# Gating the experts' rows at their copy-out, and six macro tiles of the shared expert inside the last three attention steps

## The reference, cut to what matters

```python
x = x + attention(layernorm(x))          # 16 heads of 8, window 64, rotary positions
xf = layernorm(x)                        # what follows works on xf
shared = (silu(xf @ sg) * (xf @ su)) @ sd
# router: 4 of 8 groups, then 4 of 32 experts for each token, by l2-normed centroids and a bias
gates = softmax(top_scores)              # 4 gates a token
# each expert takes at most 640 (token, choice) pairs, in token order; later ones are dropped (keep = 0)
h = silu(buf @ wg[e]) * (buf @ wu[e])    # buf: the 640 slots of expert e
out_e = h @ wd[e]
routed[token] += out_e[slot] * gate * keep
x = x + shared + routed
```

## Time and profile before

| what | value |
|---|---|
| median of 3 runs | 727.87 us (726.16 to 729.05) |
| span of the profiled execution, which is its own time here | 904.6 us, mean granted TensorE clock 0.829 |
| busy: PE, PEld, DVE, ACT, POOL | 724.0, 563.5, 534.0, 360.9, 415.1 us |
| instructions | 24570 |
| stages of the profiled execution | start to 63 us; attention to 514.4; drain steps 33, 34, 35 to 525.8, 532.8, 539.4; two macro tiles to 552.8; experts to 837.2; two late macro tiles beside the last scatter to 847.4; results and four macro tiles to 904.6 |

### The profile page before, as it was taken

One profiled execution on the slowest core, in us unless ns is written; L12 is line 12 of the kernel. 1 busy time (PEld: TensorE's weight loads), 2 busy tenths in 40 slices (PEclk: granted clock), 3 DMA queues, 4 the chain that ended last, 5 costly groups with the idle time before them and its releaser, 6 DMA issues.

```text
span 904.6 us, 24570 instructions
## 1 busy us (share of the span) xinstructions
PE 724.0 (80%) x7521; PEld 563.5 (62%) x7521; DVE 534.0 (59%) x2192; ACT 360.9 (40%) x853; POOL 415.1 (46%) x548
## 2 busy tenths in 40 slices
PE   3798888988978788898888858888888888877960
PEld 1565656665646565575665637777777777777540
DVE  3476756556577676656666656545454454543598
ACT  4465544454455445444454423332323232322200
POOL 4125343353343434334344350555555555556555
PEclk9698776676798878767788859999999999998985
DMA  8991000000000000000000002423233333421355
GB/s 268 358 390 35 14 20 15 12 23 12 12 22 10 20 9 15 10 7 14 6 7 6 6 8 84 125 76 105 76 114 107 114 115 103 126 75 32 122 182 167
DMA packets 52338, 68.37 MB, mean 76 GB/s; under 512 B 9505, under 2 KB 31807, under 8 KB 52304
## 3 DMA queue, kind: packets, MB, share of 16 engines
q1 hardware_dynamic: 38240, 53.56, 18.4%
q0 software_dynamic: 9216, 11.97, 4.4%
q10 hardware_dynamic: 4848, 2.40, 0.9%
HBM read 34.89 MB, written 39.99 MB: 83 GB/s over the span
## 4 chain that ended last, share of the span: by engine, by line
PE 52%; another core or an unknown queue 19%; issue 10%; DVE 10%; ACT 6%; POOL 1%; ACTq 1%; DVEq 1%; POOLq 0%
PE bank L693 9%; PE bank L864 7%; PE bank L680 6%; PE bank L674 5%; PE bank L663 5%; PE bank L657 3%; PE bank L701 3%; DVE x_all L1246 3%; DVE mx L1044 2%; PE bank L733 2%; ACT hact L607 2%; PE bank L817 2%; PE bank L756 1%; PE bank L747 1%
## 5 line engine op out<-in xcount | busy, mean ns | idle before, releaser
L463 POOL DMA_INDIRECT pair_results<-yout,yidx x160 | 157.2, 982 | 143.4 <-ACT yout L625 104.0
L447 POOL DMA_INDIRECT expert_slots<-xfe,sidx x128 | 127.0, 992 | 141.5 <-DVE sidx L1148 108.3
L864 PE MATMUL bank<-xgT_parts,wgu_parts 128*128 128x320 f32 x768 | 147.2, 344 | 46.4 <-ACT hact L607 46.4
L864 PEld LDWEIGHTS bank<-xgT_parts,wgu_parts 128*128 128x128 f32 x768 | 125.9, 208 | 57.3 <-ACT hact L607 50.3
L519 ACT ACTIVATE pt<-bank 128x512 f32<-128x512 f32 x128 | 76.2, 596 | 182.2 <-PE bank L680 164.9
L1259 DVE TENSOR_TENSOR hact<-hact,bank 128x320 f32<-128x320 f32 x128 | 57.1, 481 | 140.2 <-ACT hact L607 133.1
L1044 DVE TENSOR_REDUCE mx<-bank 128x4 f32<-128x512 f32 x128 | 87.3, 683 | 32.5 <-PE bank L663 19.7
L421 POOL TENSOR_TENSOR pout<-pin,mhalf 128x3 f32<-128x3 f32 (+2 forms) x36 | 29.9, 830 | 127.4 <-DVE pin L970 127.4
L890 PE MATMUL bank<-wdn,hact 128*128 128x128 f32 x640 | 82.7, 288 | 2.3 <-issue 2.3
L890 PEld LDWEIGHTS bank<-wdn,hact 128*128 128x128 f32 x640 | 82.5, 207 | 2.5 <-issue 2.5
L623 ACT COPY yout<-bank 128x512 f32<-128x512 f32 x32 | 18.7, 585 | 162.2 <-remote 151.0
(11 more groups left out here) (148 smaller groups left out, 1335.1 us busy)
## 6 DMA issues: line engine op xcount, KB each, us to landing
expert_slots<-fill SPq DMA_DIRECT2D x32, 322.5 KB, 6.5
xg<-expert_slots SPq DMA_DIRECT2D x32, 322.5 KB
pair_results<-rload SPq DMA_DIRECT2D x32, 256.0 KB
rload<-pair_results SPq DMA_DIRECT2D x16, 512.0 KB, 4.0
wgu<-in_L_ffn_wg_dram SPq DMA_DIRECT2D x32, 128.0 KB
wgu<-in_L_ffn_wu_dram SPq DMA_DIRECT2D x32, 128.0 KB
wdn<-in_L_ffn_wd_dram SPq DMA_DIRECT2D x32, 128.0 KB
pair_results<-yout,yidx POOLq DMA_INDIRECT x160
```

The lines of the kernel that those rows point to most:

```text
L447: g.indirect_dma_start(out=slots_d, out_offset=bass.IndirectOffsetOnAxis(ap=sidx[:, tr.b, k:k + 1], axis=0), in_=xfe[:, tr.b, k, :], in_of ...
L463: g.indirect_dma_start(out=pairs_d, out_offset=bass.IndirectOffsetOnAxis(ap=yidx[:, c, j:j + 1], axis=0), in_=yout[:, c, j, :], in_offset= ...
L864: last = mm(bank[2 + 2 * w + h][:, 0:CH], wgu_parts[:, e.b, wp, w, h * P:(h + 1) * P], xgT_parts[:, e.b, xp, ch * CH:(ch + 1) * CH], start ...
```

## The change

The gate moves from the end of the kernel to the experts' copy-out. The rows in the slot buffer get one more column (ROW = 130), the gate of the pair, which VectorE writes where it wrote the table of gates before; the scatter to the slots waits for it. In an expert's step ScalarE does five activations of 128x128 with the gate as scale per row in place of two copies, each with its own semaphore count; GpSimd waits, in front of each of its five scatters, for that one part. The copy of the pair numbers (and now gates) on VectorE moves from the head of the step to its end. At the end GpSimd does one addition of 128x512 a pair of tiles and VectorE two of 128x256.

Six of the eight macro tiles move into the drain, two in each of the steps 33 to 35, with single PSUM banks for gate (0), up (1) and down (5), placed between the attention and routing work of each engine. The other two stand where the early ones stood. None is left behind the experts.

```diff
...
 SPAN = P + WIN
-ROW = D + 1
+ROW = D + 2
 OOB = float(1 << 20)
...
 CH = cap // 2
-SHARED_EARLY = 2
+SHARED_DRAIN = 6
 NR = 8
-CSTEPS = 5
-COMB_EARLY = 4 * (N // 512 - SHARED_EARLY - 2)
+CSTEPS = 2
...
 xfT_all = sb("xfT_all", [P, N])
-gates = sb("gates", [P, NT, TOPK])
...
 yout = sb("yout", [P, 2, ST, D])
-ypair = sb("ypair", [P, 2, ST])
+ypair = sb("ypair", [P, 2, ST, 2])
...
 rload = sb("rload", [P, NR, TOPK, D])
-gates_late = sb("gates_late", [P, NR, 2])
...
       tile_of((m - 1) // 2, (m - 1) % 2) if m > start else None)
+def drain_macro(tau, i):
+  if isinstance(tau, int) and NT < tau < NT + 4:
+    return tile_of(tau - NT - 1, i)
+  return None
...
     sp.dma_start(xg[:, c].rearrange("p j c -> p (j c)"), slots_v[e]).then_inc(xg_arrived[c], 16)
-  sp.wait_ge(S.fill_done, 2)
+  sp.wait_ge(S.fill_done, 3)
...
   g.memset(fill[:, :, 0:D], 0.0).then_inc(S.fill_done, 1)
-  g.memset(fill[:, :, D:ROW], OOB).then_inc(S.fill_done, 1)
+  g.memset(fill[:, :, D:D + 1], OOB).then_inc(S.fill_done, 1)
+  g.memset(fill[:, :, D + 1:ROW], 0.0).then_inc(S.fill_done, 1)
...
       hold(pool)
-      g.tensor_copy(xfe[:, tw.b, :, D:ROW], pair[:, bass.ds(tw.n, 1), :].rearrange("p o k -> p k o"))\
+      g.tensor_copy(xfe[:, tw.b, :, D:D + 1], pair[:, bass.ds(tw.n, 1), :].rearrange("p o k -> p k o"))\
...
       pool.wait_ge(S.xf_copied, tr.n + 1)
+      pool.wait_ge(S.gate_done, 2 * tr.n + 2)
...
       pool.wait_ge(S.yidx_ready, e + 1)
-      pool.wait_ge(S.y_evac, 2 * e + 2)
-      hold(pool)
       for j in range(ST):
+        pool.wait_ge(S.y_evac, ST * e + (j + 1))
+        hold(pool)
...
           oob_is_err=False).then_inc(y_sent[c], 16)
-  pool.wait_ge(S.gate_done, 2 * NT)
...
       tiles = slice(2 * c, 2 * c + 2)
-      g.tensor_copy(gates_late[:, tiles, :], gates[:, bass.ds(2 * q, 2), 2:TOPK])\
-      .then_inc(S.late_gates, 1)
       pool.wait_ge(r_arrived[c], 16 * (i + 1))
-      pool.wait_ge(S.late_gates, q + 1)
       hold(pool)
-      g.tensor_tensor(rload[:, tiles, 2:TOPK, :], rload[:, tiles, 2:TOPK, :],
-              gates_late[:, tiles, :].unsqueeze(3).broadcast_to([P, 2, 2, D]), ALU.mult)\
-      .then_inc(S.late_gated, 1)
-      pool.wait_ge(S.late_gated, q + 1)
-      g.tensor_tensor(rload[:, tiles, 2, :], rload[:, tiles, 2, :], rload[:, tiles, 3, :], ALU.add)\
-      .then_inc(S.late_sum, 1)
+      g.tensor_tensor(rload[:, tiles, 0:2, :], rload[:, tiles, 0:2, :], rload[:, tiles, 2:TOPK, :],
+              ALU.add).then_inc(S.half_sum, 1)
...
   def step(tau, tn, tf, tp, ts, tw, tr):
+    def drain_silu(i, h):
+      m = drain_macro(tau, i)
+      if m is not None:
+        act.wait_ge(S.sh_gu, 4 * m.n + (2 * h + 1))
+        wait(act, S.sh_down, m.n - 1)
+        a.activation(sact[:, m.b, h], bank[0][:, :], ACT.Silu).then_inc(S.sh_act, 1)
...
       a.copy(xfT[:, tr.b], bank[4][:, 3 * D:3 * D + P]).then_inc(S.xfT_evac, 1)
+    drain_silu(0, 0)
...
       .then_inc(S.xf_copied, 1)
+    drain_silu(0, 1)
...
       a.copy(oT[:, tw.b], bank[3][:, 0:P]).then_inc(S.oT_evac, 1)
+    drain_silu(1, 0)
     exponentials(0)
...
     exponentials(3)
+    drain_silu(1, 1)
...
         a.activation(sact[:, m.b, h], bank[h][:, :], ACT.Silu).then_inc(S.sh_act, 1)
-  shared_steps(shared_step, 0, SHARED_EARLY)
+  shared_steps(shared_step, SHARED_DRAIN, N // 512)
...
       wait(act, y_sent[ed.b], 16 * ST * ed.half)
-      a.copy(yout[:, ed.b, 0:4], bank[6][:, :].rearrange("p (j d) -> p j d", d=D))\
-      .then_inc(S.y_evac, 1)
-      a.copy(yout[:, ed.b, 4:ST], bank[7][:, 0:D].rearrange("p (j d) -> p j d", d=D))\
-      .then_inc(S.y_evac, 1)
+      act.wait_ge(S.ypair_ready, ed.n + 1)
+      hold(act)
+      for j in range(ST):
+        a.activation(yout[:, ed.b, j], bank[6 + j // 4][:, j % 4 * D:(j % 4 + 1) * D], ACT.Copy,
+              scale=ypair[:, ed.b, j, 1:2]).then_inc(S.y_evac, 1)
...
   lagged_steps(act, expert_step, NE, True)
-  shared_steps(shared_step, SHARED_EARLY, N // 512)
...
       last.then_inc(S.qkT_done, 1)
+    def drain_gate_up(i, h):
+      m = drain_macro(tau, i)
+      if m is None:
+        return
+      cols = slice(h * P, (h + 1) * P)
+      if m.n == 0 and h == 0:
+        pe.wait_ge(S.w_loaded, 16 * 3)
+        pe.wait_ge(S.p1_reduced, NU * NT)
+        pe.wait_ge(S.mT_evac, NT)
+        pe.wait_ge(S.qT_evac, NT)
+      pe.wait_ge(S.xfT_kept, 4 * m.n + 4)
+      wait(pe, S.sh_act, 2 * m.n + h)
+      mm(bank[0][:, :], sgw[:, cols], xfT_all[:, bass.ts(m.n, 512)], start=True, stop=True)\
+       .then_inc(S.sh_gu, 1)
+      wait(pe, S.sh_mul, 2 * m.n + h)
+      mm(bank[1][:, :], suw[:, cols], xfT_all[:, bass.ts(m.n, 512)], start=True, stop=True)\
+       .then_inc(S.sh_gu, 1)
+    def drain_down(i):
+      m = drain_macro(tau, i)
+      if m is None:
+        return
+      pe.wait_ge(S.sh_mul, 2 * m.n + 2)
+      wait(pe, S.sh_added, m.n)
+      for j in range(4):
+        for h in range(2):
+          last = mm(bank[5][:, j * D:(j + 1) * D], sact[:, m.b, h, j * P:(j + 1) * P], sdw[:, h, :],
+               start=(h == 0), stop=(h == 1))
+      last.then_inc(S.sh_down, 1)
...
        .then_inc(S.xfT_done, 1)
+    drain_gate_up(0, 0)
...
         pe.wait_ge(S.centT_evac, 1)
+    drain_gate_up(0, 1)
...
       first_scores(0)
+    drain_gate_up(1, 0)
...
       mm(bank[3][:, P:2 * P], oT[:, tw.b], wout[:, :], start=True, stop=True).then_inc(S.wout_done, 1)
+    drain_down(0)
...
       second_scores(3)
+    drain_gate_up(1, 1)
...
       last.then_inc(S.pvT_done, 1)
+    drain_down(1)
   attention_steps(pe, step)
-  pe.wait_ge(S.w_loaded, 16 * 3)
...
       last.then_inc(S.sh_down, 1)
-  shared_steps(shared_step, 0, SHARED_EARLY)
-  pe.wait_ge(S.sh_added, SHARED_EARLY)
+  pe.wait_ge(S.sh_act, 2 * SHARED_DRAIN)
+  pe.wait_ge(S.sh_mul, 2 * SHARED_DRAIN)
+  shared_steps(shared_step, SHARED_DRAIN, N // 512)
+  pe.wait_ge(S.sh_added, N // 512)
...
       pe.wait_ge(S.h_mul, 4 * ed.n + 4)
-      wait(pe, S.y_evac, 2 * ed.n)
+      wait(pe, S.y_evac, ST * ed.n)
...
   lagged_steps(pe, expert_step, NE, True)
-  pe.wait_ge(S.h_act, 4 * NE)
-  pe.wait_ge(S.h_mul, 4 * NE)
-  shared_steps(shared_step, SHARED_EARLY, N // 512)
...
       dve.wait_ge(S.gate_done, 2 * tr.n + 1)
-      v.scalar_tensor_tensor(gates[:, bass.ds(tr.n, 1), :].rearrange("p o k -> p (o k)"), ex4[:, tr.b],
-                 exr[:, :], keep[:, :], ALU.mult, ALU.mult).then_inc(S.gate_done, 1)
+      v.tensor_scalar(xfe[:, tr.b, :, D + 1], ex4[:, tr.b], exr[:, :], None, ALU.mult)\
+      .then_inc(S.gate_done, 1)
+    def drain_times(i, h):
+      m = drain_macro(tau, i)
+      if m is not None:
+        dve.wait_ge(S.sh_act, 2 * m.n + (h + 1))
+        dve.wait_ge(S.sh_gu, 4 * m.n + (2 * h + 2))
+        v.tensor_tensor(sact[:, m.b, h], sact[:, m.b, h], bank[1][:, :], ALU.mult)\
+        .then_inc(S.sh_mul, 1)
+    def drain_add(i):
+      m = drain_macro(tau, i)
+      if m is not None:
+        dve.wait_ge(S.sh_down, m.n + 1)
+        xs = x_all[:, bass.ds(4 * m.n, 4), :]
+        v.tensor_tensor(xs, xs, bank[5][:, :].rearrange("p (t d) -> p t d", d=D), ALU.add)\
+        .then_inc(S.sh_added, 1)
     def at(tile, operation, *args):
...
     at(tr, masked_a)
+    drain_times(0, 0)
     at(tp, maxima, 0)
     at(tr, masked_b)
+    drain_times(0, 1)
     at(tw, add_attention)
...
     at(tr, marks_b)
+    drain_times(1, 0)
     at(tw, length_a)
...
     at(tp, maxima, 3)
+    drain_add(0)
     at(tr, positions_a)
...
     at(tr, slots_c)
+    drain_times(1, 1)
+    drain_add(1)
...
       .then_inc(S.sh_added, 1)
-  shared_steps(shared_step, 0, SHARED_EARLY)
+  shared_steps(shared_step, SHARED_DRAIN, N // 512)
   def combine(q, c, turn):
-    dve.wait_ge(r_arrived[c], 16 * (turn + 1))
+    dve.wait_ge(S.half_sum, q + 1)
+    xp = x_all[:, bass.ds(2 * q, 2), :]
     for k in range(2):
-      for h in range(2):
-        t = 2 * q + h
-        xt = x_all[:, bass.ds(t, 1), :].rearrange("p o d -> p (o d)")
-        if k:
-          dve.wait_ge(S.comb_step, CSTEPS * q + (h + 1))
-        gk = gates[:, bass.ds(t, 1), k:k + 1].rearrange("p o k -> p (o k)")
-        v.scalar_tensor_tensor(xt, rload[:, 2 * c + h, k], gk, xt, ALU.mult, ALU.add)\
-        .then_inc(S.comb_step, 1)
-    dve.wait_ge(S.comb_step, CSTEPS * q + 4)
-    dve.wait_ge(S.late_sum, q + 1)
-    xp = x_all[:, bass.ds(2 * q, 2), :]
-    v.tensor_tensor(xp, xp, rload[:, 2 * c:2 * c + 2, 2], ALU.add).then_inc(S.comb_step, 1)
+      if k:
+        dve.wait_ge(S.comb_step, CSTEPS * q + 1)
+      v.tensor_tensor(xp, xp, rload[:, 2 * c:2 * c + 2, k], ALU.add).then_inc(S.comb_step, 1)
...
       wait(dve, y_sent[ed.b], 16 * ST * ed.half)
-      v.tensor_copy(yidx[:, ed.b], ypair[:, ed.b]).then_inc(S.yidx_ready, 1)
+      v.tensor_copy(yidx[:, ed.b], ypair[:, ed.b, :, 0]).then_inc(S.yidx_ready, 1)
...
       dve.wait_ge(xg_arrived[en.b], 16 * (en.half + 1))
-      wait(dve, S.yidx_ready, en.n - 1)
-      v.tensor_copy(ypair[:, en.b], xg[:, en.b, :, D]).then_inc(S.ypair_ready, 1)
...
```

(20 more changed lines are left out.)

## The result

| kernel | median of runs | ratio to before, 95% interval |
|---|---|---|
| before, same series | 727.01 us (723.26 to 729.05) | |
| changed | 739.59 us (736.60 to 741.43) | 1.0188 (1.0140 to 1.0235) |
| changed, a second time, before 726.13 | 736.55 us (731.49 to 743.08) | 1.0114 (1.0066 to 1.0161) |

The change makes the kernel slower, by 12.6 us here and by 10.4 us in the second measurement; the forecast was 736.0, +8.2. Both intervals lie above 1. The experiments were run in three series, each on a chip of its own: in one the kernel before took 912.42 us, about what the profiled execution in front of the prediction took (904.6), and in the others 727.37 and 726.13, so kernels are compared only with kernels of the same series.

A forecast was written before the change was run, and what follows sets the result against it. The prediction took VectorE to bound the end and its routing chain the drain, TensorE holding 52% of the profiled chain. Sum: 26.3 - 0.9 - 16.7 - 0.5 + 0 = +8.2 on 727.9, 736 us; range 716 to 756.

The forecast's parts named there:

- mechanism A: Rival forecast as slower: the drain pays more than the end gets back; 736 us, chance 0.5.
- The drain, +26.3: Steps 33 to 35 with six macro tiles inserted: 51.3 us against 25.0, floor 45, ceiling 60.
- The two tiles behind it, -0.9: Two macro tiles between drain and expert loop: 12.5 us where 13.4 stood.
- The combination, -16.7: End of the kernel: 16 pairs at 2.1 us, 33.6 us against 50.3; bounds on the gain 10 to 23.
- The six tiles out of the end, nothing by themselves: End: TensorE was covered by VectorE and the last scatter, so removing 31 us of matmuls gives nothing back by itself.
- The first scatter, -0.5: Last scatter before the end starts after the first of five copy-outs, about 0.5 us earlier.
- The loop, 0: Expert loop: five activations cost 0.2 to 0.7 us more an expert, hidden; waits and earlier scatter taken as nothing.
- the cover of 2.5 us: Expert loop: next gate matmuls come 2.5 us after the down matmuls, silu done at 1.5 to 1.9; without cover 6 to 22 us.
- B: Rival, faster: loop turns with the copy-out, earlier first scatter saves 0.4 an expert, 13 us, giving 723; chance 0.22.
- C: Rival, no change: drain at its floor +20, a pair at 1.8 us, giving 725; chance 0.1.
- D: Rival, much slower: loop waits on GpSimd or ScalarE's parts on the path cost 0.5 an expert, +16, 752; chance 0.18.
- The gap of 172 us: Expert loop: 19% of the profiled 904.6 us on an unknown queue; timed loop argued to run at 6.3 to 7 us an expert.

The follow-up runs named there:

- the second profile: The kernel before, unchanged, profiled again: 731.39 us in one run, span 729.6; the changed kernel was also profiled a second time, in another series.
- the ring of eight: The changed kernel with eight buffers of two tiles for the results in place of four: 914.23 us, ratio 1.0004 to the kernel before at 912.42.
- the gate part alone: Kernel before with only the gate at the copy-out and plain additions, macro tiles as before: 709.96 us, ratio 0.9767; again 713.03, 0.9802.
- the drain part alone: Kernel before with only the six macro tiles moved into the last three attention steps, old gates and combination: 750.27 us, ratio 1.0319.
- the four kernels with the gate part: On the 912.42 us chip: reordered change 909.82 us, larger ring 914.23, gate part with no early macro tile 892.80, with one 893.25.
- reordered: Changed kernel with VectorE's first product ahead of the scores, last ahead of the second positions: 909.82 us, ratio 0.9966; other chip 731.49, 1.0075.
- the one wait: The changed kernel with one wait for all five copy-out parts in place of one each: 739.49 us, ratio 1.0198 to the kernel before.

## Why the prediction was right, step by step

The forecast was slower, 736.0 us, by mechanism A; it came out slower by the same mechanism, at 739.59 and 736.55, within the range.

**The drain, +26.3.** Measured +28.8, 52.2 us (20.3, 15.5, 16.4) where 51.3 (19.5, 16.5, 15.3) was worked out. The products behind the routing chain are where the prediction put them. In step 33 the load of the table for the exponentials stands at 412.64, and TensorE waits 1.36 us behind it. The drain has seven loads at 1.28 us, as forecast; the eighth of the profile stands at the start of the kernel. The larger difference is in what the old steps took: 23.4 us in the second profile, not 25.0. The ceiling's condition, the first macro tile of each step at 1.2 GHz, didn't occur: the granted clock was 1.00, 1.00 and 0.92. A part of it did in the second profile, where one gate and one up pair of step 33 took 2.07 and 1.91 us in place of 1.13 and 1.02, and the three steps took 54.7 us.

**The two tiles behind it, -0.9.** Measured -2.6: 11.8 us, where before they ran at a mean clock of 0.79.

**The combination, -16.7.** From the first multiply-add to the last addition it was 49.6 us before (677.5 to 727.1) and is 33.4 after (699.5 to 732.9), so -16.2. Mechanism and size part here. The sum had 1.04 for GpSimd, 0.86 for VectorE and 0.2, in turns, 2.1 us a pair. GpSimd's addition takes 1.26 us, as the 1.04 was that of the multiplication, and VectorE's 0.85 for two, and these do overlap; what makes 2.1 a pair is the ring, put at 1.7 because the loads were taken to land in 4.0 us. They land in 5.5 (with that and the 1.26, the prediction's own sum for the ring gives 2.15), and that the ring of eight shortens the stage bears it out. That the 2.1 held is luck: the bound was another one. The stage as a whole gave back less, 13.9, for two things that were left out. The first pair has to pass GpSimd before VectorE can begin, 5.2 us from the first load's issue (694.3 to 699.5), where before VectorE's multiply-adds began after 3.7 (673.8 to 677.5). And behind the last addition there are 3.4 us where there were 2.5.

**The six tiles out of the end, nothing by themselves.** Right within 1.2 us beside the gate part; with the old combination, the whole end gave back 3.5. The cover was richer than the prediction made use of: 12 us of scatters behind the loop, and, once the combination is plain additions, the half of it in which VectorE is idle.

**The first scatter, -0.5.** Not seen: the last scatters take 12.18 us against 11.86.

**The loop, 0.** Right. Five activations take 1.40 us, 0.65 more than the two copies, inside the +0.2 to +0.7, and TensorE doesn't wait for them. The activation with its scale by a pointer takes 372 ns, where the estimate without it was 290, so 82 ns more. The Trainium skill ("ScalarE: Activation LUTs", What ACT_TABLE_LOAD costs) gives about 93 ns for a pointer operand, and the trace, with that estimate, agrees to about 10 ns. The 15 us that the prediction worked out from it for the path didn't come: no loop with the gate part is longer than that of before. That the cover of 2.5 us is what hid it is argued. The single profiles give 217.5 us for the loop of before, 215.7 for the change, 213.0 and 214.5 for the gate part alone, 212.3 for the drain part alone, which can't be told apart from each other.

**The rivals.** B needs copy-out and scatter to follow each other. In the runs that the forecast was about they don't: GpSimd's scatters follow each other there with gaps of 0.30 us. On the chip of 912 us they do, and there the four kernels with the gate part have loops of 279.0 to 279.6 us, against 284.4 in the earlier trace rows: 5 us, 0.16 an expert, not 0.4, and between single profiles. C needed a drain at its floor of 45 us and a pair at 1.8; the drain had 52.2, and even reordered 46.5 (399.3 to 445.8). D fell with the one wait, and its other half, ScalarE's parts on the path, with the gate part's loop of 213.0 us.

**The gap of 172 us.** The prediction argued that the long turns belonged to the profiled execution alone. The conclusion for the timed loop was right, 6.8 us an expert. But the long turns aren't a matter of one recording: on one chip every run of the kernel before, 23 of them, took 901 to 924 us, and the profiles from there have such turns (8.6 us). The sign that the prediction named, turns of some 8.5 us in the profile of the changed kernel, didn't show on the chip of 727 us, where they take 6.7. On which chip the execution of 904.6 us ran isn't on record.

**What didn't stand in it:** step 32, which ran at 15.25 us with a clock of 0.66 in the second profile of before and at 11.2 with 1.00 in the change. That is 4.0 of the spans' difference in favour of the change, but it belongs to neither part: the gate part alone shows 11.15 in one profile and 15.0 in the other. The second profile of before, at 731.39, was also 4.0 above its median, so against the median the change's loss is nearer to 10.7 than to 6.7.

## What to carry to other kernels

Work that lies under a bound engine isn't freed by moving it, and once another edit relieves that engine, its old place is cheaper still: ask of two edits made together whether they draw on the same idle time, and time each alone. Before filling idle time on one engine, look at the engine whose chain makes that time, and put the inserted work's steps on it ahead of the chain; that gave back 5 of some 28 us here, since 31 us of matmuls don't fit into 11 us of gaps in any order. A ring is sized by the landing time, and one profile isn't enough for it: the same loads of the kernel before landed in 4.0 us (median) in its first profile and in 5.8 in its second.
